# A cross-attention and mixture-of-experts block: inputs laid out turned, LayerNorms and routing placed inside the attention, expert chunks unrolled

## The chip, the cores and the metric

One core of one Trainium2 chip. A kernel is a fixed program of five engines: PE (TensorE, matmuls), DVE (VectorE), ACT (ScalarE), POOL (GpSimd) and SP (SyncE, which here issues the DMAs). The metric is the device time of one execution in microseconds (us), smaller is better.

## The reference, cut to what matters

```
x: (16, 256, 128)   ctx: (16, 1601, 96)   16 heads of 64, E = 32 experts, top 4
n   = layernorm(x)
q,k,v = n @ Wq, ctx @ Wk, ctx @ Wv                  # per head
x   = x + softmax(q k^T / 8) v @ Wo + bo
t   = layernorm(x)                                  # 4096 tokens
s   = sigmoid(t @ router_weight.T)
c   = s + router_bias; the best 2 of 4 groups (sum of their two largest), then the best 4 experts
w   = s[chosen] / sum(s[chosen]) * 2.5
x   = x + sum_e w[e] * down_e(silu(gate_e t) * up_e t) + shared expert
```

## The kernel before, in words

All of it is fp32; products that need precision are made of three fp32r matmuls, each operand being split into a high part (`hi`, a copy rounded to fp32r) and the rest (`lo`, full minus high). Wq and Wk are multiplied into one matrix A (128 x 96) per head, Wv and Wo into one matrix B, so that scores are n A ctx^T.

*Head.* x and the first two batches' keys are loaded; PE turns (transposes) the keys and the weights, makes A and B, DVE takes the LayerNorm of all 32 token tiles (lines 979 to 1003), and the 32 maxima tiles of the first group are made (L577) and reduced (L1038).

*Attention.* 64 groups (16 batches x 4 groups of 4 heads, 1024 queries). A group has 13 key tiles ("steps"). At step t PE makes the scores of tile t (6 matmuls of 512 columns, L608 to L614), then side jobs, then the weighted values of tile t-2 (6 matmuls, L623 to L629), then side jobs. ACT takes two exponentials of each score tile (L875, L878), and the rest `p_lo` (L282, two inputs in SBUF) is taken by DVE, at steps 3, 5, 7 and 9 by POOL. A side job fills one of only two PSUM banks (`side`) and DVE (or ACT and DVE) empties it: PE may fill a bank for job j only when job j-2 has been drained (`s_drain`). The table `SLOTS` sets the order: M, 32 maxima tiles of the group to come (L577, 402 columns; DVE reduces each, L1038); C, a quarter of the next batch's keys turned (L526, split by ACT L813 and DVE L1013); Y, a head's output projected (L637) and added to x1 (L1053, L1058); T, the maxima turned; Q, queries of a later group. Each engine's stream is in order. POOL also copies and splits A and x for a coming group (L421 to L430) and the values (L438, L440).

*Transition.* After the attention the expert weights are loaded, DVE and ACT take the second LayerNorm, PE turns the tokens (L520) and makes the router logits (L716), then 51 weight matrices are turned (L734) and split (L925, L1228), with the routing of chunk 0 (L1157 to L1218) in between.

*Expert chunks.* 8 chunks of 512 tokens, a loop over 17 pairs of experts q (the first is the shared expert). For each, PE makes gate and up (3 matmuls each, L745 to L747), spreads the routing weights (L790) and makes `down(q-2)` (3 matmuls, each of these 512 columns); ACT takes silu (L949), DVE two products (L1260, L1263), ACT `h_hi` (L932), POOL `h_lo` (L503), which `down` waits for. `hid`, `h_hi` and `h_lo` have three slots. DVE also routes the next chunk between the products at q = 5, 7, 9, 11, 13 and 15; PE turns these weights at the start of the next chunk (L768).

Of the kernel before, what the change touches and what calls it, by code (L numbers as in the profile page):

```python
# [10 lines left out]
I32 = mybir.dt.int32  # L29
# [8 lines left out]
def xattn_moe(nc, x, ctx, Wq, Wk, Wv, Wo, bo, router_w, router_b, gate_w, up_w, down_w,  # L38
              sh_gate_w, sh_up_w, sh_down_w, out):
    B, NQ, D = x.shape  # L40
    _, NC, DC = ctx.shape
    INNER = Wq.shape[1]
    DH = 64
    H = INNER // DH
    E, EI, _ = gate_w.shape
    SCALE = float(DH) ** -0.5
    assert D == P and NQ == 2 * P and H == 16 and EI * 2 == P and sh_gate_w.shape[0] == P
# [8 lines left out]
    QT = 4  # L56
    SPAD = NGB * QT
    MAXW = 402
    DOUBLES = 4 * MAXW - NC
    NM = 4 * (GQ // P)  # L60
    T = B * NQ // P
    NCH = T // 4
    NP = E // 2 + 1
    YW = D + 1
    OW = DC + 1

    stack = ExitStack()
    with stack:
# [6 lines left out]

        x1 = sb(stack, "x1", [P, T + 2, D])
        ident = sb(stack, "ident", [P, P])
        bo_rows = sb(stack, "bo_rows", [P, D])
        stats = sb(stack, "stats", [P, T, 6])
        mean = sb(stack, "mean", [P, T])  # L80
        dif = sb(stack, "dif", [P, T])
        var = sb(stack, "var", [P, T])
        std = sb(stack, "std", [P, T])
        rstd = sb(stack, "rstd", [P, T])
        xn = sb(stack, "xn", [P, 2, 4, D])
        recip = sb(stack, "recip", [P, 2])


        att = ExitStack()
        xnT = sb(att, "xnT", [P, (B + 1) * NQ])  # L90
        A_all = sb(att, "A_all", [P, H, DC])
        B_all = sb(att, "B_all", [OW, H, YW])
        A_hi = sb(att, "A_hi", [P, GH, DC], F32R)
        A_lo = sb(att, "A_lo", [P, GH, DC], F32R)
        x_hi = sb(att, "x_hi", [P, NQ], F32R)
        x_lo = sb(att, "x_lo", [P, NQ], F32R)
        pool_spare = sb(att, "pool_spare", [P, 1])
        nat = sb(att, "nat", [P, 2, SPAD, DC])
        c_stage = sb(att, "c_stage", [P, QT, DC])
        cT_hi = sb(att, "cT_hi", [OW, 2, SPAD * P], F32R)  # L100
        cT_lo = sb(att, "cT_lo", [DC, 2, SPAD * P], F32R)
        v_hi = sb(att, "v_hi", [P, 2, SPAD, OW], F32R)
        v_lo = sb(att, "v_lo", [P, 2, SPAD, OW], F32R)
        qT_hi = sb(att, "qT_hi", [OW, 2, GQ], F32R)
        qT_lo = sb(att, "qT_lo", [DC, 2, GQ], F32R)
        qT_max = sb(att, "qT_max", [DC, GQ], F32R)
# [3 lines left out]
        oT = sb(att, "oT", [OW, GQ])  # L110
        with ExitStack() as early:
            Wq_sb = sb(early, "Wq_sb", [P, INNER])
            Wk_sb = sb(early, "Wk_sb", [DC, INNER])
            Wv_sb = sb(early, "Wv_sb", [DC, INNER])
            Wo_sb = sb(early, "Wo_sb", [P, INNER // P, D])
            WT = sb(early, "WT", [P, 2, 3, P])
# [5 lines left out]

        moe = stack.enter_context(ExitStack())
        x2T_hi = sb(moe, "x2T_hi", [P, T * P], F32R)
        x2T_lo = sb(moe, "x2T_lo", [P, T * P], F32R)
        x2T_f = sb(moe, "x2T_f", [P, 2, BANK])
        w_nat = sb(moe, "w_nat", [P, 3, NP, P])
        gu_hi = sb(moe, "gu_hi", [P, 2, NP, P], F32R)
        gu_lo = sb(moe, "gu_lo", [P, 2, NP, P], F32R)
        d_hi = sb(moe, "d_hi", [P, NP, P], F32R)  # L130
        d_lo = sb(moe, "d_lo", [P, NP, P], F32R)
        rw_nat = sb(moe, "rw_nat", [E, D])
        rwT = sb(moe, "rwT", [P, E])
        rb_rows = sb(moe, "rb_rows", [P, E])
        before = sb(moe, "before", [P, N_EGROUP, N_EGROUP])
        sel_plain = sb(moe, "sel_plain", [P, E // 2, P])
        sel = sb(moe, "sel", [P, E // 2, P], F32R)
        score = sb(moe, "score", [P, T + 4, E])
        choice = sb(moe, "choice", [P, 4, E + TOP_K])
        struck = sb(moe, "struck", [P, 4, E + TOP_K])  # L140
        top8 = sb(moe, "top8", [P, 4 * N_EGROUP, 8])
        best8 = sb(moe, "best8", [P, 4, 8])
        g_sum = sb(moe, "g_sum", [P, 4, N_EGROUP])
        g_more = sb(moe, "g_more", [P, 4, N_EGROUP, N_EGROUP])
        g_same = sb(moe, "g_same", [P, 4, N_EGROUP, N_EGROUP])
        g_keep = sb(moe, "g_keep", [P, 4, N_EGROUP])
        ra = sb(moe, "ra", [P, 4, E])
        sigmoid = sb(moe, "sigmoid", [P, 4, E])
        spare = sb(moe, "spare", [P, 1])
        r1 = sb(moe, "r1", [P, 4])  # L150
        w_cat = sb(moe, "w_cat", [P, 4, P])
        w_r = sb(moe, "w_r", [P, 4, E], F32R)
        wT = sb(moe, "wT", [P, T * P], F32R)
        act_g = sb(moe, "act_g", [P, 2, BANK])
        gu_mul = sb(moe, "gu_mul", [P, 2, BANK])
        hid = sb(moe, "hid", [P, 3, BANK])
        h_hi = sb(moe, "h_hi", [P, 3, BANK], F32R)
        h_lo = sb(moe, "h_lo", [P, 3, BANK], F32R)
        yT = sb(moe, "yT", [P, BANK])

# [5 lines left out]
        s_x = sem("x_landed")  # L166
        s_w = sem("attn_weights_landed")
        s_nat = [sem("context_landed_even"), sem("context_landed_odd")]
        s_id = sem("identity_ready")
        s_set = sem("padding_preset")  # L170
        s_pset = sem("constants_preset")
# [47 lines left out]
        s_si = sem("gate_activated")  # L219
        s_hd = sem("hidden_made")  # L220
# [1088 lines left out]
```

## Time and profile before

| | us |
|---|---|
| median of 3 runs | 3518.87 (3518.13 to 3519.88) |
| the profiled execution | 3519.92 |
| its span, first to last instruction | 3518.1 |
| PE busy | 3410.5 |
| DVE busy | 2505.3 |
| ACT busy | 2027.8 |
| POOL busy | 1163.7 |

The program runs on one core, so the profile shows the whole time but 1.8 us. Busy shares are averages over stages that have different limits; the stages are read one by one from windows of the trace. "PEclk" is the clock granted to TensorE as a share of the full one.

### The profile page before, as it was taken

What the parts mean: (1) busy time and instruction counts of PE and PEld (TensorE: products, weight loads), DVE (VectorE), ACT (ScalarE), POOL (GpSimd) and SP (SyncE); (2) the same over time, 40 slices, a digit from 0 to 9 for tenths busy, and PEclk for the clock granted to TensorE, in tenths of its full rate; (3) what the DMA queues carried; (4) which work ended last, traced back from release to release, by engine and by line L of the source; (5) the groups of instructions that cost most, each with busy time, mean ns of one, the idle gap of its engine ahead of it and who ended that gap; (6) DMA issues with size and microseconds to landing.
All of it is one profiled execution on the core that took longest, in us unless ns stands there. A gap on an engine that the chain in (4) does not pass through costs nothing.

```text
span 3518.1 us, 54934 instructions
## 1 busy us (share of the span) xinstructions
PE 3410.5 (97%) x15929; PEld 2660.0 (76%) x15929; DVE 2505.3 (71%) x4705; ACT 2027.8 (58%) x2452; POOL 1163.7 (33%) x953
## 2 busy tenths in 40 slices
PE   6999999999999999999999999999999999979888
PEld 4777777777777777777777777777777777766665
DVE  5777776776776777677777767777767767778887
ACT  3566666566556666665666665665666665544443
POOL 3333332333333332323333332333333323324444
PEclk9999999999999999999999999999999999979999
DMA  2000000000000000000000000000000000020000
GB/s 67 0 0 8 0 8 0 8 0 8 0 8 0 8 0 8 0 8 0 3 5 0 8 0 8 0 8 0 8 0 8 0 8 0 3 37 6 6 6 6
DMA packets 18022, 22.31 MB, mean 6 GB/s; under 512 B 2976, under 2 KB 14280, under 8 KB 17928
## 3 DMA queue, kind: packets, MB, share of 16 engines
q1 hardware_dynamic: 17928, 20.86, 2.2%
q8 instruction: 83, 1.36, 0.2%
q14 instruction: 11, 0.09, 0.0%
HBM read 18.49 MB, written 2.10 MB: 6 GB/s over the span
## 4 chain that ended last, share of the span: by engine, by line
PE 83%; issue 8%; POOL 5%; DVE 2%; ACT 1%; DVEq 0%; POOLq 0%; DMA 0%; SPq 0%; ACTq 0%
PE side L577 12%; PE op L623 11%; PE op L629 11%; PE op L626 11%; PE st L608 10%; PE st L611 10%; PE st L614 10%; POOL h_lo L503 5%; PE side L637 3%; DVE cT_lo L1013 1%; PE side L569 1%; PE side L526 1%; PE side L571 1%; PE side L570 1%; ACT cT_hi L813 1%
## 5 line engine op out<-in xcount | busy, mean ns | idle before, releaser
L1038 DVE TENSOR_REDUCE m_part<-side 128x1 f32<-128x402 f32 x2064 | 1105.0, 571 | 513.1 <-PE side L577 503.0
L875 ACT ACTIVATE p_full<-st 128x1024 f32<-128x1024 f32 (+1 forms) x832 | 855.7, 1028 | 911.8 <-PE st L614 911.8
L282 POOL TENSOR_TENSOR p_lo<-p_full,p_hi 128x1024 fp32r<-128x1024 f32 x256 | 657.6, 2569 | 1060.6 <-ACT p_hi L878 1060.6
L282 DVE TENSOR_TENSOR p_lo<-p_full,p_hi 128x1024 fp32r<-128x1024 f32 (+1 forms) x576 | 717.9, 1246 | 220.3 <-ACT p_hi L878 220.3
L878 ACT ACTIVATE p_hi<-st 128x1024 fp32r<-128x1024 f32 (+1 forms) x832 | 853.7, 1026 | 0.0
L577 PE MATMUL side<-cT_hi,qT_max 96*128 96x402 f32 x2064 | 619.5, 358 | 7.4 <-DVE qT_lo L1032 2.0
L608 PE MATMUL st<-qT_hi,cT_hi 97*128 (+3 forms) x1668 | 540.6, 405 | 1.9 <-ACT p_hi L878 1.0
L623 PE MATMUL op<-p_hi,v_hi 128*97 128x512 f32 (+1 forms) x1664 | 526.4, 397 | 0.0
L611 PE MATMUL st<-qT_lo,cT_hi 96*128 (+3 forms) x1668 | 524.9, 396 | 0.0
L629 PE MATMUL op<-p_hi,v_lo 128*97 128x512 f32 (+1 forms) x1664 | 520.6, 394 | 0.0
L626 PE MATMUL op<-p_lo,v_hi 128*97 128x512 f32 (+1 forms) x1664 | 520.6, 394 | 0.0
L577 PEld LDWEIGHTS side<-cT_hi,qT_max 96*128 96x128 f32 x2064 | 389.4, 189 | 173.3 <-DVE cT_lo L1013 28.3
L614 PE MATMUL st<-qT_hi,cT_lo 96*128 (+3 forms) x1668 | 518.4, 392 | 0.0
L611 PEld LDWEIGHTS st<-qT_lo,cT_hi 96*128 96x128 f32 (+1 forms) x1668 | 308.9, 185 | 79.5
L614 PEld LDWEIGHTS st<-qT_hi,cT_lo 96*128 96x128 f32 (+1 forms) x1668 | 306.6, 184 | 80.7
L629 PEld LDWEIGHTS op<-p_hi,v_lo 128*97 128x97 f32 (+1 forms) x1664 | 269.8, 162 | 116.3 <-issue 0.2
L626 PEld LDWEIGHTS op<-p_lo,v_hi 128*97 128x97 f32 (+1 forms) x1664 | 269.7, 162 | 114.9
L608 PEld LDWEIGHTS st<-qT_hi,cT_hi 97*128 97x128 f32 (+1 forms) x1668 | 295.9, 186 | 31.3 <-issue 4.5
L623 PEld LDWEIGHTS op<-p_hi,v_hi 128*97 128x97 f32 (+1 forms) x1664 | 266.1, 164 | 29.5
L503 POOL TENSOR_TENSOR h_lo<-hid,h_hi 128x512 fp32r<-128x512 f32 x136 | 175.0, 1287 | 251.7 <-ACT h_hi L932 250.3
L434 POOL COPY c_stage<-nat 128x384 f32 (+1 forms) x68 | 34.8, 512 | 650.7 <-PE side L571 642.4
L813 ACT ACTIVATE cT_hi<-side 96x512 f32 (+1 forms) x68 | 40.3, 594 | 257.0 <-PE side L526 257.0
(182 smaller groups left out, 3242.2 us busy)
## 6 DMA issues: line engine op xcount, KB each, us to landing
nat<-in_ctx SPq DMA_DIRECT2D x18, 576.0 KB
out_x<-x SPq DMA_DIRECT2D x8, 256.0 KB, 2.3
qT_hi<-m_row SPq DMA_DIRECT2D x65, 4.0 KB
w_nat<-in_L_ffn_gate_w SPq DMA_DIRECT2D x2, 512.0 KB, 7.2
w_nat<-in_L_ffn_up_w SPq DMA_DIRECT2D x2, 512.0 KB, 9.4
Wq_sb<-in_L_xattn_Wq SPq DMA_DIRECT2D x1, 512.0 KB, 6.2
Wo_sb<-in_L_xattn_Wo SPq DMA_DIRECT2D x1, 512.0 KB, 9.4
nat<-in_ctx SPq DMA_DIRECT2D x18, 24.4 KB
```

Of the source, the lines that this page charges most:

```text
L282: eng.tensor_tensor(p_lo[0:m, slot(s), :], p_full[0:m, s % 2, :], p_hi[0:m, slot(s), :].bitcast(F32), ALU.subtract).then_inc(s_lo_pool if ...
L503: pool.tensor_tensor(h_lo[:, q % 3, :], hid[:, q % 3, :], h_hi[:, q % 3, :].bitcast(F32), ALU.subtract).then_inc(s_hl, 1)
L577: pe.matmul(where[:, 0:MAXW], qT_max[:, tile * P:(tile + 1) * P], cT_hi[0:DC, par, part * MAXW:(part + 1) * MAXW], start=True, stop=True). ...
L608: pe.matmul(st[0:m, s % 2, j, :], cT_hi[:, par, keys], qT_hi[:, i % 2, halves[j]], start=True, stop=False)
L611: pe.matmul(st[0:m, s % 2, j, :], cT_hi[0:DC, par, keys], qT_lo[:, i % 2, halves[j]], start=False, stop=False)
L614: mm = pe.matmul(st[0:m, s % 2, j, :], cT_lo[:, par, keys], qT_hi[0:DC, i % 2, halves[j]], start=False, stop=True)
L623: pe.matmul(op[0:OW, j, :], v_hi[0:m, par, s, :], p_hi[0:m, slot(s), halves[j]], start=(s == 0), stop=False)
L626: pe.matmul(op[0:OW, j, :], v_hi[0:m, par, s, :], p_lo[0:m, slot(s), halves[j]], start=False, stop=False)
L629: mm = pe.matmul(op[0:OW, j, :], v_lo[0:m, par, s, :], p_hi[0:m, slot(s), halves[j]], start=False, stop=(s == S - 1))
L875: act.activation(p_full[0:m, s % 2, :], both(st[0:m, s % 2]), ACT.Exp, scale=SCALE)
L878: act.activation(p_hi[0:m, slot(s), :], both(st[0:m, s % 2]), ACT.Exp, scale=SCALE).then_inc(s_ex, 1)
L1038: dve.tensor_reduce(m_part[:, k:k + 1], where[:, 0:MAXW], AX.X, ALU.max).then_inc(s_drain, 1)
```

## The change

The function is rewritten in many places. What is computed stays the same.

- *Layout.* The host passes x as 128 x 32 x 128, the keys twice (plain, and turned with seven keys repeated so that four pieces of 402 columns hold them), the attention weights and the expert weights already turned and side by side, and takes the output in the layout of x1.
- *Head.* Only the first two token tiles are normalised there. A is made for all heads and split once (`A_hi`, `A_lo` for 16 heads), so POOL stages no A later. The first maxima are made in pairs of banks and reduced two at a time, with the products of later heads in between. No keys and no weights are turned on PE.
- *Attention.* `qT_max` is gone: maxima use `qT_hi`. Keys of the next batch come turned; POOL copies and splits them with the values (`split_piece`, four instructions a group). The C job is replaced by `EXTRA`: nothing in group 0, L (turn the next batch's two token tiles) in group 1, N (turn two token tiles for the second LayerNorm, those of the batch before) in group 2, R (router logits) in group 3. DVE gets `between(t)`: statistics in groups 0 and 1 at t = 7, normalising in groups 1 and 2 at t = 3, the routing of 256 tokens in group 3 at t = 6, 7, 8 and 10. The root of the variance is taken by POOL (`pow`). ACT's part of the extra job stands behind exp(5) rather than ahead of it. All engines' loops hold 8 groups unrolled.
- *Transition.* Only the last batch's second LayerNorm and its logits are left; the first five experts' weights were loaded before the attention loop.
- *Expert chunks.* Fully unrolled, `down` is made three experts late (`down(g - 3)`), four slots (`hslot`), no routing on DVE but that of the last 256 tokens in chunk 1. In chunk 0, ACT and DVE split one expert's three matrices (128 x 384) at each q, two ahead. The routing weights of the next chunk are turned at q = 10.

```diff
-        SLOTS = {2: ("MM", "M"), 3: ("MM", "M"), 4: ("MM", "MM"), 5: ("MM", "MC"), 6: ("MM", "MM"),
+        PLACES = {2: ("MM", "M"), 3: ("MM", "M"), 4: ("MM", "MM"), 5: ("MM", "MX"), 6: ("MM", "MM"),
...
+        EXTRA = ("", "L", "N", "R")
...
+            def split_piece(bb, par, i):
...
+                pool.tensor_copy(cT_hi[0:DC, other, cols], keys_tur[:, cols])
+                pool.tensor_copy(v_hi[:, other, tiles, 0:DC], keys_nat[:, tiles, :]).then_inc(s_sh, 1)
...
+                pool.tensor_tensor(cT_lo[:, other, cols], keys_tur[:, cols],
+                                   cT_hi[0:DC, other, cols].bitcast(F32), ALU.subtract)
+                pool.tensor_tensor(v_lo[:, other, tiles, 0:DC], keys_nat[:, tiles, :],
+                                   v_hi[:, other, tiles, 0:DC].bitcast(F32), ALU.subtract).then_inc(s_v, 1)
...
+            def token_stats(tiles, base=0):
+                for q in range(2):
+                    ins = dve.bn_stats(stats[:, q, :], x1[:, tiles[q], :])
+                link(ins, base)
+                carry()
+                for q in range(2):
+                    ins = dve.bn_aggr(moments[:, q, :], stats[:, q, :])
+                link(ins, base)
+                dve.tensor_scalar(var_eps[:, :], moments[:, :, 1], EPS, None, ALU.add).then_inc(s_var, 1)
+
+            def normalise(tiles, count):
+                dve.wait_ge(s_rstd, count)
+                for q in range(2):
+                    ins = dve.tensor_scalar(xn[:, q, :], x1[:, tiles[q], :], moments[:, q, 0:1], rstd[:, q:q + 1],
+                                            ALU.subtract, ALU.mult)
...
+            def add_one(count):
+                dve.wait_ge(s_ls, count)
+                dve.tensor_scalar(ra[:, :, :], ex[:, :, :], 1.0, None, ALU.add).then_inc(s_drain, 1)
...
+            def route_groups(base=0):
+                flat = g_sum[:, :, :].rearrange("p t g -> p (t g)")
+                link(dve.tensor_tensor(flat, top8[:, :, 0], top8[:, :, 1], ALU.add), base)
...
+                def between(t):
+
+                    if i == 0 and t == 7:
+                        token_stats([dve.snap(bb * 4 + (2 * par + 4 + q)) for q in range(2)], links)
+                    elif i == 1 and t == 3:
+                        normalise([dve.snap(bb * 4 + (2 * par + 4 + q)) for q in range(2)], bb * 4 + (2 * par + 2))
+                    elif i == 1 and t == 7:
+                        token_stats([dve.snap(bb * 4 + (2 * par + q)) for q in range(2)], links)
+                    elif i == 2 and t == 3:
+                        normalise([dve.snap(bb * 4 + (2 * par + q)) for q in range(2)], bb * 4 + (2 * par + 3))
+                    elif i == 3 and t == 6:
+                        route_scores(jobs + (job_at[i]["R"][0] + 1), links)
+                    elif i == 3 and t == 7:
+                        route_groups(links)
+                    elif i == 3 and t == 8:
+                        route_experts(links)
+                    elif i == 3 and t == 10:
+                        route_weights(bass.ds(bb * 4 + 2 * par, 2), links)
+
+                at = places(i)
                 lo(0)
                 for t in range(2, S):
-                    side_jobs(SLOTS[t][0])
+                    side_jobs(at[t][0])
                     lo(t - 1)
                     if t == S - 1:
                         lo(t)
-                    side_jobs(SLOTS[t][1])
+                    between(t)
+                    side_jobs(at[t][1])
...
+            for c in range(NCH):
                 for q in range(NP):
-                    w = (q - 1) % NP
...
+                    if g >= 3:
+                        down(g - 3)
```

## Rows read from the trace of the kernel before

**Rows 1.** The page, first part: busy time of each engine.

```profile
PE 3410.5 (97%) x15929; PEld 2660.0 (76%) x15929; DVE 2505.3 (71%) x4705; ACT 2027.8 (58%) x2452; POOL 1163.7 (33%) x953
```

**Rows 2.** Windows by stage: us, busy of PE, PEld, DVE, ACT, POOL, clock.

```profile
0.00:79.10 79.10, 48.55 (x194) 33.45 (x194) 41.92 (x115) 22.89 (x70) 28.87 (x37) 1.00 0.23 67
79.10:3070.60 2991.50, 2984.35 (x14157) 2340.36 (x14158) 2110.02 (x3746) 1816.24 (x2052) 951.01 (x768) 1.00 0.01 4
3070.60:3129.50 58.90, 35.16 (x169) 30.94 (x169) 41.41 (x133) 22.50 (x43) 8.80 (x12) 0.61 0.34 57
3129.50:3518.10 388.60, 342.41 (x1414) 255.25 (x1412) 311.99 (x712) 166.16 (x288) 174.98 (x136) 0.98 0.02 6
```

**Rows 3.** Waits of the whole span: total us, times, longest.

```profile
PEld side L577 <- DVE cT_lo L1013: 28.3, 64, 0.5
PEld side L577 <- DVE m_part L1038: 27.4, 111, 0.3
```

**Rows 4.** Chain of waits in one attention group: start, us, what.

```profile
1544.02 0.44 PE side L526 x4
...
1545.86 0.18 PE side L577
...
1546.08 0.45 PE side L577
```

**Rows 5.** Timeline of DVE in two attention groups.

```profile
1503.21 1.06 DVE L1038 TENSOR_REDUCE m_part<-side 128x1 f32<-128x402 f32 x2 [0.70 <-PE side L577]
1504.19 1.50 DVE L282 TENSOR_TENSOR p_lo<-p_full,p_hi 128x1024 fp32r<-128x1024 f32 x1
...
1536.40 1.21 DVE L282 TENSOR_TENSOR p_lo<-p_full,p_hi 128x1024 fp32r<-128x1024 f32 x1
```

**Rows 6.** Timeline of POOL, attention and transition.

```profile
1503.86 0.74 POOL L430 TENSOR_TENSOR x_lo<-xnT,x_hi 128x256 fp32r<-128x256 f32 x1
1505.12 2.81 POOL L282 TENSOR_TENSOR p_lo<-p_full,p_hi 128x1024 fp32r<-128x1024 f32 x1 [0.53 <-ACT p_hi L878]
...
1537.34 2.53 POOL L282 TENSOR_TENSOR p_lo<-p_full,p_hi 128x1024 fp32r<-128x1024 f32 x1 [4.87 <-ACT p_hi L878]
...
3077.39 4.47 POOL L493 TENSOR_SCALAR_AFFINE_SELECT sel_plain<-sel_plain 128x2048 f32<-128x2048 f32 x2
```

**Rows 7.** Single lines: instructions, ns min/median/max, first and last start, forms.

```profile
L1170 DVE TENSOR_TENSOR g_sum<-top x9: 186/944/944, 3118.0 to 3482.4; 128x16 f32<-128x16 f32 x9
...
L1003 DVE TENSOR_SCALAR xn<-x,mean,rstd x64: 335/341/348, 39.1 to 3103.8; 128x128 f32 x64
...
L1214 DVE CAST w_r<-ra x9: 217/862/867, 3128.0 to 3505.0; 128x128 fp32r<-128x128 f32 x9
...
L768 PE MATMUL op<-ident,w_cat x32: 272/273/447, 3128.8 to 3460.4; 128*128 128x128 f32 x32
```

**Rows 8.** Timeline of DVE between attention and expert chunks.

```profile
3074.71 0.87 DVE L979 BATCH_NORM_STATS2 stats<-x 128x6 f32<-128x128 f32 x4
...
3079.87 2.03 DVE L990 TENSOR_SCALAR var<-var 128x32 f32<-128x32 f32 x1
...
3120.03 0.23 DVE L1180 TENSOR_TENSOR g_more<-g_more,g_same 128x64 f32<-128x64 f32 x1
3120.29 0.22 DVE L1181 TENSOR_REDUCE g_keep<-g_more 128x16 f32<-128x64 f32 x1
```

**Rows 9.** Chain of waits in the head: start, us, what.

```profile
54.96 0.21 PE side L570
...
60.00 15.57 DVE m_part L1038 x32
```

**Rows 10.** Timeline of PE in the expert chunks and at the end.

```profile
3137.30 0.39 PE L745 MATMUL st<-x2T_hi,gu_hi 128*128 128x512 f32 x1
...
3139.59 0.39 PE L745 MATMUL st<-x2T_hi,gu_hi 128*128 128x512 f32 x1
...
3510.72 0.79 PE L745 MATMUL op<-h_hi,d_hi 128*128 128x512 f32 x1 [2.65 <-POOL h_lo L503]
```

More of the change, by code:

```diff
@@ L28 @@
 F32R = mybir.dt.float32r
-I32 = mybir.dt.int32
 P = 128
@@ new lines, in project_queries @@
+            def project_queries(where, g, half, k):
+                for h in range(2):
+                    head = g * GH + 2 * k + h
+                    o = where[0:DC, h * NQ:(h + 1) * NQ]
+                    pe.matmul(o, A_hi[:, head, :], x_hi[:, half, :], start=True, stop=False)
+                    pe.matmul(o, A_hi[:, head, :], x_lo[:, half, :], start=False, stop=False)
+                    mm = pe.matmul(o, A_lo[:, head, :], x_hi[:, half, :], start=False, stop=True)
+                mm.then_inc(s_fill, 1)
@@ L604, in scores @@
+            pe.wait_ge(s_mc, 1)
+            pe.wait_ge(s_drain, J0_T - 1)
+            turn_maxima(bank(J0_T))
+            def scores(s, slot, par):
                 m = rows(s)
@@ L664, in side_jobs @@
                         k = made[kind]
-                        j = job_at[kind][k]
+                        j = job_at[i][kind][k]
                         made[kind] += 1
+                        where = bank(jobs0 + j)
                         pe.wait_ge(s_drain, jobs + (j - 1))
@@ new lines, in _ @@
+            for k in range(2):
+                queries_lo(bank(J0_Q + k), k + 1, k, 0)
+            for u in range(NM // 2):
+                where = (st[:, 0], st[:, 1], op)[u % 3]
+                tile, part = u % (NM // 4), u // (NM // 4) * 2
+                if u == NM // 2 - 2:
+                    for k in range(2):
+                        queries_lo(bank(J0_Q1 + k), k + 3, k, 1)
+                dve.wait_ge(s_mx, u + 1)
+                dve.tensor_reduce(m_part[:, tile * 4 + part:tile * 4 + part + 2], where[:, :, 0:MAXW], AX.X,
+                                  ALU.max).then_inc(s_mxd, 1)
@@ L1239, in _ @@
-            keep_weights(None)
+                    between(t)
+                    side_jobs(at[t][1])
+            links_per_turn = 48
+            with dve.Fori(0, B // 2) as bb:
+                for par in range(2):
+                    for i in range(NGB):
+                        body(bb, par, i)
+            assert steps[0] - head_steps == links_per_turn, steps[0] - head_steps
+            steps[0] = head_steps + B // 2 * links_per_turn
+            for h in range(GH):
+                dve.wait_ge(s_drain, JOBS_END + h)
+                add_head(bank(JOBS_END + h), JOBS_END + h + 1, NG * GH + h + 1, (T, T + 1))
@@ L1282, in body @@
-                per_chunk[0] = steps[0] - start
-            per_chunk = [0]
-            chunks(dve, body)
+                    if c == 1:
+                        if q == 8:
+                            route_scores(JOBS_END + GH + 2)
+                        elif q == 10:
+                            route_groups()
+                        elif q == 12:
+                            route_experts()
+                        elif q == 14:
+                            route_weights(slice(T, T + 2))
@@ L1297 @@
     from concourse.bass_utils import run_bass_kernel_spmd
[L1299 to L1305 removed]
+    take = lambda name: np.asarray(inputs[name])
@@ new lines @@
+    flat = lambda a: np.ascontiguousarray(a, dtype=np.float32)
+    x, ctx = take("x"), take("ctx_768")
+    Wq, Wk, Wv, Wo = (take("L0_xattn_" + n) for n in ("Wq", "Wk", "Wv", "Wo"))
+    gate, up, down = (take("L0_ffn_" + n) for n in ("gate_w", "up_w", "down_w"))
+    shared = [take("L0_ffn_shared_" + n) for n in ("gate_w", "up_w", "down_w")]
+    keys = np.zeros((16, 13 * P, 96), np.float32)
+    keys[:, 0:1601] = ctx
+    attn_w = np.concatenate([Wq.T.reshape(8, P, P), Wk.T.reshape(8, P, 96), Wv.T.reshape(8, P, 96),
+                             Wo.reshape(8, P, P)], axis=2)
```

1407 lines of the change are left out of this document (641 added, 766 removed).

## The prediction

> **What bounds the kernel now.** I read the page's busy times first: PE is busy 97% of the span [rows 1]. The windows by stage say where it isn't: the head takes 79.1 us, the attention 2991.5, the transition 58.9 and the expert chunks 388.6 [rows 2]. In the attention PE is busy 2984 of 2991 us, one group of the 64 taking 2991.5/64 = 46.74. There every stall of PE is lost time and every matmul saved is won. The waits and the chain show three small stalls per group: the C job (28.3/64 = 0.44, behind DVE's cT_lo) and a late DVE reduction (27.4/64 = 0.43 [rows 3]), besides one for the heads that stays. So DVE, at 2110 us busy, is nearly in the way at some steps though its share is only 71%.
>
> **Head.** Before, DVE's 32 reductions take 15.6 us and end at 75.6; scores start at 79.1 [rows 2, 9]. After, only two tiles are normalised, the keys and weights come turned. I walk it: data at about 4, statistics and root to 5.7; normalising, turning and splitting to 10 (2.8 later if POOL's long memset of a constant row blocks DVE, which I take at half); A and the first queries to 16; then PE, not DVE, bounds the maxima: 32 tiles of 402 columns at 0.21 us per 256 [rows 9] are 10.7, three rounds of weight products 6.3, the second queries 2.6; then 3.5 to 4.5 for the maxima's row, as now (79.1 - 75.6). Together 41.0 (37 to 46): **38.1 saved**. The products' 2.1 a round is an estimate from the same rate.
>
> **Attention, work of PE.** C costs 0.44 of PE [rows 4] and its stall 0.44 (the pair behind it takes 0.45 where two singles of 0.18 would do, and waits once more [rows 4]). The stall by the late reduction has a cause: DVE's p_lo of step 6 takes 1.50 instead of 1.21 because POOL's x_lo runs until 1504.6 [rows 5, 6]; POOL no longer stages x, so 0.30 goes. A bare group is 46.74 - 0.45 - 0.44 - 0.30 = 45.55. L and N add 0.23 each (two turns of 128 columns), R about 0.45: a batch is 4 x 45.55 + 0.91 = 183.1, before 187.0. POOL's four key copies lie beside PE, and their neighbours on DVE read PSUM.
>
> **Attention, DVE's new work.** This is where it is decided. With two banks, PE's second M of a pair waits until DVE has drained the pair's forerunner. Between two pairs PE has 6 x 0.23 = 1.39 of other matmuls, a pair lasts 0.37: half a step is 1.76. DVE needs 1.06 for a pair [rows 5] and 1.21 for a p_lo, which on even t stands with POOL or nowhere and on odd t makes 2.27 in one half and 1.06 in the other. On odd t the slack behind p_lo is about 0.2; on even t it is 1.1. What `between` adds beyond that stalls PE one for one.
>
> What its pieces cost: small operations with a wait start 0.26 apart [rows 8], 0.24 at half size. Statistics: two at 0.24 (0.87 for four [rows 8]), a memset, two aggregations at about 0.15 (no row; 0.1 to 0.3), one tensor_scalar: 1.2. Groups of the routing: 7 operations, 1.7. Scores of the routing 1.6, experts 1.15, weights 1.9 (their forms for four tiles, each reduced to two). Normalising: 0.55.
>
> On top comes a lock. g_sum takes 0.19 alone and 0.94 in the median case, when POOL is in its h_lo [rows 7]; a tensor_scalar that takes 0.18 alone took 2.03, until POOL's select had ended (3077.39 + 4.47 = 3081.86 [rows 6, 8]). So such operations wait for the end of POOL's instruction. In the attention POOL's p_lo lasts 2.4 to 2.8. At t = 3 and 7 it becomes ready while DVE is in its own p_lo: 1537.34 against an end at 1537.5, 1505.12 against 1505.6 [rows 5, 6]. POOL thus goes first, and what DVE has next waits 2.4.
>
> - Group 3, t = 7, route_groups: g_sum waits to 10.2 after scores(6) began, the last of seven ends at 11.9, the reduction at 12.45, while PE wants its bank at 8.9: 3.6, and 0.3 for the second, **3.9**. Certain kind of wait: the very operation is in the rows.
> - Group 3, t = 6, 8 and 10: 0.45 + 0 + 0.5; and add_one, a tensor_scalar, behind p_lo(5): 0.7 more. With t = 7: **5.5** (4.8 without the lock on add_one).
> - Groups 0 and 1, t = 7, statistics: the last tensor_scalar waits for p_lo(7): 2.35 each (1.0 without): **4.7**.
> - Groups 1 and 2, t = 3, normalising: 2.3 each (0 without): **4.6**. Is it an operation that waits? It takes 0.335 [rows 7]. A copy of as many elements takes 0.217, which waits (0.86 [rows 7]); two scalars from memory at about 0.06 each (an estimate) bring 0.217 to 0.335. A pass at one element a cycle would give 0.40. I take it as one that waits.
>
> Sum 14.8 a batch (4.3 if nothing waited). After: 16 x (183.1 + 14.8) = 3166.4, **174.9 more** than 2991.5.
>
> What the rows show is that DVE waits for POOL's instruction to end. The Trainium skill, SBUF — State Buffer, section Who interferes with whom, speaks against this change: VectorE and GpSimd share a port pair under an exclusive lock, taken by copy, cast and tensor_scalar in their two-port mode and by operations with two SBUF inputs against a GpSimd instruction that reads SBUF. The trace agrees (2.03 and 0.94 above). By this rule both the statistics' last operation and normalising would wait, which is the sum here; had the rule only held for two tensor inputs, the sum would be that of the second rival.
>
> **Transition.** Of 58.9 [rows 2] only the last batch is left: heads added 4.1, statistics and root 1.5, normalising between POOL's memset and x2_lo 2.7, turns, logits and routing turn 3.2 at the slow clock: 11.5 (9 to 14). **47.4 saved.** The first weights are there; the rest has 6 us before its first use.
>
> **Expert chunks.** Chunks start (3460.4 - 3128.8)/7 = 47.4 apart [rows 7], but an undisturbed step takes 3139.59 - 3137.30 = 2.29 [rows 10]: 17 steps and two turns of 0.45 are 39.7. The rest is DVE's routing, late products, and `down` waiting for h_lo. The routing goes and `down` is a step later, so PE bounds: from the gate of a step to h_lo takes 5.3, `down` now comes at 8.5. In chunk 0 ACT has 1.7 and DVE 1.9 per step against 2.29: covered, if DVE's splitting fits ahead of POOL's h_lo (0 to 10 if not). 136 steps 309, turns 6, slow clock at the start 2, less three late downs 2, end of the last step to the last byte 11, stalls in chunks 0 and 1 3: 329 (324 to 338). **59.6 saved.**
>
> **The sum.** 41.0 + 3166.4 + 11.5 + 329.0 = 3547.9 against a span of 3518.1: +29.8. The profiled execution is 3519.92, 1.8 above its span; the median 3518.87 is 1.05 lower. Forecast 3518.9 + 29.8 = 3548.7, own range 3520 to 3580.
>
> **Rivals.**
> 1. *Normalising does not wait* (one port, or DVE gets it first; the margin at t = 3 is 0.2 us [rows 5, 6]). 16 x 4.6 = 73.6 less: 3475, faster. It decides from half that gain on: with a stall under 0.4 per piece the kernel is no slower. Chance 0.20.
> 2. *No one-source operation waits*, or PE's slack is larger than I read: stalls 6.8 instead of 14.8, 128 less: 3421; with no lock at all, 3381. For it: only two such rows met POOL's select, none its p_lo. Chance 0.19.
> 3. *The long stalls bring TensorE's clock down.* After 2.65 idle a matmul of 512 columns takes 0.79 instead of 0.39 [rows 10]; the 3.9 of group 3 is longer, though ahead of it PE is dense. Eleven matmuls 0.2 later each are 2.3 a batch: 3586. Chance 0.13.
> 4. *The expert chunks don't get shorter*, DVE or ACT taking PE's place: 8 x 7.7 more, 3610. Against it: DVE's 1.4 and ACT's 1.2 a step. Chance 0.04.
>
> **Numbers.** The forecast's case has 0.44. Range 3435 to 3600: it leaves out most of rival 2 and rival 4. A measurement can tell about 0.2%, 7 us. Slower by more: most of 0.44 (0.36), 0.13, 0.04: 0.53. Same: 0.05. Faster: 0.19, 0.20 and 0.03 of the forecast's own case: 0.42.
>
> **What would show it.** Right: groups 0 to 3 of a batch of about 47.9, 50.4, 48.1 and 51.5 us; DVE's xn at t = 3 and var_eps near 2.4 us long, g_sum up to 2.4; PE's waits for m_part some 230 us in all; chunks 39.7 apart; scores at 41. Wrong: xn at 0.34 throughout, or waits for m_part under 100 us; a head over 46.

## The result, and the profile after

The changed kernel takes 3603.57 us (median of 4 runs, 3602.96 to 3609.24), the kernel before 3518.5 beside it: a ratio of 1.0245 (95% interval 1.0228 to 1.0263), so 2.3 to 2.6% slower. The forecast was 3548.7, its range 3435 to 3600. The profiled execution has a span of 3600.8 us and takes 3602.96. Its page, first the busy line, then the chain that ended last:

```profile
span 3600.8 us, 50491 instructions
...
PE 3386.3 (94%) x15589; PEld 2655.2 (74%) x15589; DVE 2578.8 (72%) x4960; ACT 1935.5 (54%) x2239; POOL 1076.8 (30%) x737
...
PE 77%; DVE 11%; issue 9%; POOL 1%; DVEq 0%; ACT 0%; POOLq 0%; DMA 0%; ACTq 0%
```

PE's share fell from 97% [rows 1] to 94%, and it is busy 24 us less: the change did take work off PE, and gave more idle time back. The windows by stage say where (head, attention, transition, chunks; columns as in [rows 2]):

```profile
0.00:38.30 38.30, 20.47 (x124) 16.34 (x124) 23.48 (x34) 10.51 (x18) 25.60 (x31) 0.96 0.51 171
38.30:3265.00 3226.70, 3042.74 (x14029) 2375.06 (x14030) 2343.36 (x4576) 1750.46 (x1905) 863.06 (x560) 0.97 0.03 8
3265.00:3275.80 10.80, 4.66 (x27) 3.60 (x27) 8.85 (x27) 3.50 (x9) 2.85 (x3) 0.79 0.56 218
3275.80:3600.80 325.00, 318.42 (x1414) 260.21 (x1412) 203.16 (x324) 171.06 (x308) 185.24 (x143) 0.99 0.02 7
```

| us | before | forecast | after | after minus forecast |
|---|---|---|---|---|
| head | 79.1 | 41.0 | 38.3 | -2.7 |
| attention | 2991.5 | 3166.4 | 3226.7 | +60.3 |
| transition | 58.9 | 11.5 | 10.8 | -0.7 |
| expert chunks | 388.6 | 329.0 | 325.0 | -4.0 |
| span | 3518.1 | 3547.9 | 3600.8 | +52.9 |

Three stages gained 152.5 us and the attention lost 235.2. All that the forecast missed lies in the attention. There a batch of four groups looks like this (windows from one group's first scores to the next one's; columns: length, PE busy, PEclk, DMA share and GB/s):

```profile
240.00:288.30 48.30, 46.39 (x219) 1.00 0.00 1
288.30:339.70 51.40, 47.75 (x220) 0.97 0.00 1
339.70:387.70 48.00, 46.00 (x220) 1.00 0.04 13
387.70:441.40 53.70, 49.68 (x222) 0.94 0.05 14
```

Over all 16 batches the four groups take 48.1, 51.6, 48.0 and 53.8 in the mean, where the forecast had 47.9, 50.4, 48.1 and 51.5. Groups 0 and 2 are right to 0.2. Groups 1 and 3 are 1.2 and 2.3 longer, and they are the two in which the granted clock is below 1.

**The lock is there as forecast.** DVE in group 1 at t = 7, with POOL beside it:

```profile
314.84 1.21 DVE L1004 TENSOR_TENSOR p_lo<-p_full,p_hi 128x1024 fp32r<-128x1024 f32 x1
315.97 0.48 DVE L848 BATCH_NORM_STATS2 stats<-x 128x6 f32 x2
316.49 0.18 DVE L852 BATCH_NORM_AGGREGATE moments<-stats 128x2 f32<-128x6 f32 x1
...
316.77 1.54 DVE L854 TENSOR_SCALAR var_eps<-moments 128x2 f32<-128x2 f32 x1
...
315.77 2.51 POOL L383 TENSOR_TENSOR p_lo<-p_full,p_hi 128x1024 fp32r<-128x1024 f32 x1 [4.56 <-ACT p_hi L745]
```

POOL's p_lo ends at 315.77 + 2.51 = 318.28, var_eps at 316.77 + 1.54 = 318.31. The statistics run beside POOL at their usual pace; the tensor_scalar on two elements per partition doesn't. The same holds for the other pieces (a line's durations in ns, least/median/most):

```profile
L859 DVE TENSOR_SCALAR xn<-x,moments,rstd x68: 334/1616/2880, 5.3 to 3271.2; 128x128 f32 x64, 128x128 f32<-128x128 f32 x4
L854 DVE TENSOR_SCALAR var_eps<-moments x34: 169/1537/1544, 3.8 to 3269.9; 128x2 f32<-128x2 f32 x34
L917 DVE TENSOR_TENSOR g_sum<-top x17: 433/2349/2354, 213.1 to 3340.2; 128x8 f32<-128x8 f32 x17
L901 DVE TENSOR_SCALAR ra<-ex x17: 195/1881/1890, 205.1 to 3275.6; 128x64 f32<-128x64 f32 x17
```

**The low clock is what the forecast had left to a rival.** The same stretch of PE's stream, first in group 0 (the stall before it as long), then in group 1:

```profile
268.57 0.94 PE L449 MATMUL side<-cT_hi,qT_hi 96*128 96x402 f32 x2 [1.67 <-DVE m_part L1016]
269.35 0.63 PE L513 MATMUL op<-p_hi,v_hi 128*97 128x512 f32 x2
269.82 0.63 PE L516 MATMUL op<-p_lo,v_hi 128*97 128x512 f32 x2
270.29 0.63 PE L519 MATMUL op<-p_hi,v_lo 128*97 128x512 f32 x2
```

```profile
318.84 1.19 PE L449 MATMUL side<-cT_hi,qT_hi 96*128 96x402 f32 x2 [1.66 <-DVE m_part L1016]
319.82 1.05 PE L513 MATMUL op<-p_hi,v_hi 128*97 128x512 f32 x2
320.67 1.05 PE L516 MATMUL op<-p_lo,v_hi 128*97 128x512 f32 x2
321.53 0.88 PE L519 MATMUL op<-p_hi,v_lo 128*97 128x512 f32 x2
```

Pairs that start 0.47 apart in group 0 start 0.85 apart in group 1: about half speed, 1.2 instead of 2.4 GHz by the granted clock of 0.51 below. The windows of the two places in groups 1 and 3, and one right behind the first (PEclk is the figure after the count):

```profile
318.60:322.00 3.40, 3.16 (x8) 0.51 0.00 0
322.00:325.40 3.40, 3.40 (x19) 0.99 0.00 0
...
417.60:424.40 6.80, 5.68 (x16) 0.50 0.00 0
```

So a low stretch of 3.4 us in group 1 and one of 6.8 us in group 3, in each of the 16 batches. The first begins where a stall ends (318.6, the next matmul at 318.8), the second 1.1 us before its stall of 2.9 is over (417.6 against 418.7).

### The profile page after: what moved, and what is told of

It reads as the page before. It is cut to its first block, busy times and chain, and to the rows that moved or that the text cites. A ratio compares the mean times of both kernels' runs of the same rounds, so it can differ in the third digit from the quotient of the medians.

```text
span 3600.8 us, 50491 instructions
## 1 busy us (share of the span) xinstructions
PE 3386.3 (94%) x15589; PEld 2655.2 (74%) x15589; DVE 2578.8 (72%) x4960; ACT 1935.5 (54%) x2239; POOL 1076.8 (30%) x737
## 4 chain that ended last, share of the span: by engine, by line
PE 77%; DVE 11%; issue 9%; POOL 1%; DVEq 0%; ACT 0%; POOLq 0%; DMA 0%; ACTq 0%
PE side L449 10%; PE op L513 9%; PE op L516 9%; PE st L499 9%; PE op L519 9%; PE st L502 9%; PE st L505 9%; PE side L525 3%; DVE m_part L1016 3%; DVE p_lo L1004 3%; PE st L614 2%; PE st L612 2%; PE st L613 2%; DVE xn L859 1%; DVE g_sum L917 1%
## 5 line engine op out<-in xcount | busy, mean ns | idle before, releaser
L449 PE MATMUL side<-cT_hi,qT_hi 96*128 96x402 f32 x2048 | 613.1, 364 | 178.5 <-DVE m_part L1016 165.0
L449 PEld LDWEIGHTS side<-cT_hi,qT_hi 96*128 96x128 f32 x2048 | 395.0, 193 | 344.6 <-DVE m_part L1016 220.2
L499 PE MATMUL st<-qT_hi,cT_hi 97*128 97x512 f32 (+1 forms) x1668 | 548.3, 410 | 3.2 <-DMA qT_hi<-m_row 3.0
L513 PE MATMUL op<-p_hi,v_hi 128*97 128x512 f32 (+1 forms) x1664 | 540.4, 407 | 0.0
L516 PE MATMUL op<-p_lo,v_hi 128*97 128x512 f32 (+1 forms) x1664 | 533.0, 402 | 0.0
L519 PE MATMUL op<-p_hi,v_lo 128*97 128x512 f32 (+1 forms) x1664 | 532.3, 402 | 0.0
L502 PE MATMUL st<-qT_lo,cT_hi 96*128 96x512 f32 (+1 forms) x1668 | 529.5, 398 | 0.0
L505 PE MATMUL st<-qT_hi,cT_lo 96*128 96x512 f32 (+1 forms) x1668 | 523.4, 395 | 0.0
L525 PEld LDWEIGHTS side<-B_all,oT 97*128 97x128 f32 x1040 | 153.7, 200 | 28.8 <-DVE m_part L1016 12.2
L892 DVE SCALAR_TENSOR_TENSOR x<-side,recip,x 128x128 f32 (+1 forms) x520 | 158.5, 347 | 11.1 <-DVE recip L889 2.5
```

What stands on the lines that cost most here:

```text
L449: return pe.matmul(where[:, 0:MAXW], qT_hi[0:DC, slot, tile * P:(tile + 1) * P], cT_hi[0:DC, par, part * MAXW:(part + 1) * MAXW], start=Tr ...
L499: pe.matmul(st[0:m, s % 2, j, :], cT_hi[:, par, keys], qT_hi[:, slot, halves[j]], start=True, stop=False)
L502: pe.matmul(st[0:m, s % 2, j, :], cT_hi[0:DC, par, keys], qT_lo[:, slot, halves[j]], start=False, stop=False)
L505: mm = pe.matmul(st[0:m, s % 2, j, :], cT_lo[:, par, keys], qT_hi[0:DC, slot, halves[j]], start=False, stop=True)
L513: pe.matmul(op[0:OW, j, :], v_hi[0:m, par, s, :], p_hi[0:m, slot(s), halves[j]], start=(s == 0), stop=False)
L516: pe.matmul(op[0:OW, j, :], v_hi[0:m, par, s, :], p_lo[0:m, slot(s), halves[j]], start=False, stop=False)
```

## The experiments

Two theories stood after this. *Lock and clock:* the stalls come of DVE's operations that wait for POOL's p_lo, their size is as forecast, and each long one brings PE's clock down, which costs the missing 3.8 a batch. The rival: *load*, DVE simply has too much to do at those steps, or the surplus lies in the bare batch. All group times below are means over the 16 batches of the profiled execution. Executions of one kernel with such stalls differ (norm_at_4: 3497.8 to 3512.9 us with mean granted clocks of 0.985 to 0.989; the profiled one took longest, at 0.985), so a count "of 16" is that of one execution.

### no_pieces: the bare batch

```diff
                 def between(t):
+                    if (i, t) in ((0, 7), (1, 7)):
+                        dve.memset(spare[:, :], 0.0).then_inc(s_var, 1)
+                    elif (i, t) in ((1, 3), (2, 3)):
+                        dve.wait_ge(s_rstd, bb * 4 + (2 * par + (i + 1)))
+                        dve.memset(spare[:, :], 0.0).then_inc(s_xn, 1)
+                    elif (i, t) == (3, 10):
+                        dve.memset(spare[:, :], 0.0).then_inc(s_rw, 1)
+                    return
```

> Work left out: statistics, normalising and routing of all batches but the first and the last inside the attention (the operations between the steps), with constant routing weights in their place; PE's and ACT's jobs for them stay. This measures the bare batch. Theory (bare batch 183.1, 0.7 for the add_one that still waits): attention 16 x 183.8 = 2941, whole 3603.6 - 3226.7 + 2941 = 3318, and no stretch of low clock after the head. Rival (PE's slack was misread, a part of the surplus is in the bare batch): a batch of 185 to 187, 3337 to 3370.

Measured: 3331.66 us. One batch, its four groups:

```profile
406.40:452.40 46.00, 45.77 (x219) 1.00 0.01 2
452.40:498.10 45.70, 45.70 (x220) 1.00 0.00 1
498.10:543.80 45.70, 45.70 (x220) 1.00 0.05 12
543.80:590.80 47.00, 46.19 (x223) 1.00 0.06 18
```

In the mean 45.9 + 45.7 + 45.7 + 47.0 = 184.3, where the theory had 183.8, and no low clock. The attention takes 16 x 184.3 and 4.2 at its end, 2954 instead of 2941, so the forecast's removals from PE (C, its stall, the late p_lo) are right within 0.5 a batch, and 17.1 of the 201.4 of a batch of the changed kernel are the pieces' doing (their stalls and the low clock behind them). Group 3's 47.0 is R (0.45 forecast) and the add_one that waits (0.7): together 1.3 over the others.

### var_by_sum: one operation in another form

```diff
-                dve.tensor_scalar(var_eps[:, :], moments[:, :, 1], EPS, None, ALU.add).then_inc(s_var, 1)
+                dve.tensor_reduce(var_eps[:, :], moments[:, :, 1:3], AX.X, ALU.add).then_inc(s_var, 1)
```

with EPS in a third column of `moments`.

> One operation in its old place, in another form: the variance plus epsilon by a tensor_reduce over the pair (variance, epsilon) instead of a tensor_scalar. Theory 1 (a tensor_scalar waits for the end of POOL's p_lo, a reduction doesn't): var_eps takes about 0.2 instead of 1.54, the long step of groups 0 and 1 falls from 5.97 and 7.3 to about 4.6, and group 1's stretch of low clock, if it hangs on the length of that stall, goes too: 16 x (1.4 + 1.4) = 45 less, 3559, or 3538 without the low clock. Rival A (DVE has too much to do behind its p_lo, whatever the form): no change, 3603. Rival B (any operation of DVE on SBUF waits for POOL): no change, and the reduction itself is about 1.5 long.

Measured: 3563.39 us, ratio to before 1.0124 (1.0102 to 1.0146).

```profile
L854 DVE TENSOR_REDUCE var_eps<-moments x34: 156/157/158, 3.8 to 3224.3; 128x2 f32<-128x4 f32 x34
```

From 1.54 to 0.16 in the same place, beside the same POOL instruction: it is the form of the operation, not DVE's load and not the mere company of POOL. Group 0 went from 48.1 to 46.8; its long step from 5.95 to 4.61, as expected. The stall left at t = 7 is 0.9 and brings no low clock in any of the 32 groups 0 and 1. But the stall at t = 3, unchanged at 2.3, which had brought none, now does so in 4 of 16 groups 1 and in 13 of 16 groups 2, which take 49.2 instead of 48.0. That wasn't expected, and is why 3538 wasn't reached.

### norm_at_4 and stats_at_8: each half alone

```diff
-                    elif i == 1 and t == 3:
+                    elif i == 1 and t == 4:
...
-                    elif i == 2 and t == 3:
+                    elif i == 2 and t == 4:
```

> Normalising goes from t = 3 to t = 4, where DVE has no p_lo and POOL's has ended; nothing else. Theory 1 (lock): xn is 0.34 long throughout, the long step of groups 1 and 2 falls from 5.8 to 3.6 at most, 16 x 2 x 2.2 = 70 less: 3533. Rival A (DVE's own load): the stall shrinks only by p_lo's share, 0.67 - 0.2 each: 16 x 2 x 0.5 = 15 less, 3588. On the clock: if the low stretch in group 1 at t = 7 needs the stall at t = 3 before it, it goes and another 16 x 1.3 = 21 go with it (3512); if the stall at t = 7 is enough, it stays (3533).

Measured: 3503.02 us, 0.9948 of before (0.9931 to 0.9964). Two of the eight pieces that `between` places in a batch, 0.67 us each, were moved by one step: that alone turns a loss of 2.4% into a gain of 0.5%. xn's median is 0.34:

```profile
L859 DVE TENSOR_SCALAR xn<-x,moments,rstd x68: 335/341/2880, 5.4 to 3181.0; 128x128 f32 x64, 128x128 f32<-128x128 f32 x4
```

Groups: 48.5, 48.3, 45.7 and 53.0; group 2 is a bare one again, group 1 has low clock in 4 batches instead of 16 (group 0 in 3 instead of none), and group 3's low stretch is 3.4 us in 14 batches (52.9) and 6.8 in two (54.0). Load alone would have given 3588. The time is 9 us under the lower of the theory's two figures, 3512, since it had no change in group 3; why that stretch got shorter is open.

```diff
-                    if i == 0 and t == 7:
+                    if i == 0 and t == 8:
...
-                    elif i == 1 and t == 7:
+                    elif i == 1 and t == 8:
```

> The mirror of norm_at_4: only the statistics of groups 0 and 1 go from t = 7 to t = 8, normalising stays at t = 3, group 3 as in the changed kernel. Theory (lock): var_eps takes 0.17, the long steps at t = 7 of groups 0 and 1 go, the ones at t = 3 of groups 1 and 2 stay at 5.8: groups of 45.9, 48.0, 48.0 and 53.8, 16 x (2.1 + 3.6) = 91 less than 3603.6: 3513. On the clock: group 1 has one stall of 2.3 then and group 2 one. If low clock in group 1 wants two stalls in one group, neither has it (3513); if a single stall of this length can bring it, as delay_only's did in 11 of 16 batches, up to 16 x 1.5 to 3.0 more (3537 to 3560).

Measured: 3536.39 us, at the lower end of the second alternative (3537). var_eps takes 0.17 and group 0 is at 45.9: the lock's part came as expected. On the clock, one stall of 2.3 in group 1 brings it down in 14 of 16 batches, one in group 2 in 6 of 16. "Two stalls in one group" is refuted as the condition. What it gives is a clean price, the same group with and without low clock (two batches of this run, group 1; then two of group 3, with a low stretch of 3.4 and of 6.8 us):

```profile
88.30:136.30 48.00, 46.02 (x220) 1.00 0.00 1
284.20:333.70 49.50, 47.50 (x220) 0.97 0.00 1
...
579.10:631.90 52.80, 48.80 (x222) 0.97 0.05 15
184.30:238.20 53.90, 49.92 (x222) 0.94 0.05 14
```

49.5 against 48.0: 1.5 us for a stretch of 3.4. The other runs give the same: 49.53 against 47.96 (var_by_sum, group 2), 49.43 against 47.86 (delay_only, group 1). In group 3 the 9 batches with a stretch of 3.4 take 52.8 and the 7 with one of 6.8 take 53.8: the longer one costs 1.0 more, so about 2.5 in all.

### delay_only: idle time without a lock

To no_pieces is added:

```diff
+                        if i == 1:
+                            for k in range(20, 31):
+                                dve.bn_stats(scratch[:, k, :], x1[:, 2, :])
...
+                    elif (i, t) == (3, 7):
+                        for k in range(20):
+                            dve.bn_stats(scratch[:, k, :], x1[:, 2, :])
```

> Work left out as in no_pieces (statistics, normalising and routing of the batches in the attention); in their place DVE does dummy bn_stats in a row at t = 7, which wait for nothing: 11 in group 1 (11 x 0.245 = 2.7) and 20 in group 3 (4.9). Does PE's idle time alone bring its clock down, without any lock? Theory (it does): PE stalls by 2.5 and 4.7, and behind that the low clock costs as in the changed kernel, 2.3 to 3.6 a batch: a batch of 184.3 + 7.2 + 2.3 to 3.6, group 3 at 53 to 54, whole 3331 + 16 x (9.5 to 10.8) = 3483 to 3504. Rival (the low clock belongs to the lock, to POOL or to code loading): no low stretch, 3331 + 16 x 7.2 = 3446.

Measured: 3474.31 us. Groups 45.9, 48.9, 45.7 and 53.0; low clock in 11 of 16 groups 1 and in all groups 3. Two groups 1 of this run:

```profile
85.20:133.00 47.80, 46.20 (x220) 1.00 0.00 1
277.10:326.50 49.40, 47.80 (x220) 0.97 0.00 1
```

In group 1 no operation of DVE waits for POOL and none of `between`'s pieces is left (in group 3 add_one still waits, as in no_pieces): PE idle for some 2 us inside dense work is enough to bring its clock down. The whole is 9 us under the expected range, since 11 bn_stats stalled PE by 2.1, not 2.5, and 20 by about 3.9, not 4.7 (52.4 with a low stretch of 3.4, less 1.5 and 47.0), and 5 groups kept their clock.

### group3_left and even_steps: towards a better kernel

group3_left has both moves above (t = 3 to 4, 7 to 8).

> Statistics at t = 8 and normalising at t = 4 as in even_steps; group 3 (scores at 6, groups at 7, experts at 8, weights at 10) as in the changed kernel. It separates the terms of group 3 from the others' and from their clock. Theory: groups 0 to 2 as in even_steps (45.9, 45.75, 45.7); group 3 has 47.0 + 4.4 for route_groups + 0.8 for the others = 52.2 without and about 53 to 53.7 with low clock; 3346 + 16 x 4.5 to 5.9 = 3418 to 3440. If the low clock in group 3 comes from the earlier stalls of groups 1 and 2, it goes (3418); if route_groups' own stall of over 3 us is enough, it stays (3430 to 3440).

Measured: 3441.47 us. Groups 45.9, 45.8, 45.7 and 53.8:

```profile
516.90:562.60 45.70, 45.70 (x220) 1.00 0.05 12
562.60:616.60 54.00, 50.02 (x223) 0.94 0.05 15
```

Group 3 keeps its full length and its 6.8 us of low clock with no stall ahead of it in groups 0 to 2: the stall of route_groups (up to 3.4 us of idle time on PE's weight loads) is enough by itself. The run without it is even_steps, where group 3 has no low stretch.

even_steps moves group 3's pieces too, and the router's turn with them:

```diff
-        PLACES = {2: ("MM", "M"),
+        PLACES = {2: ("MM", "MZ"),
...
-        EXTRA = ("", "L", "N", "R")
+        EXTRA = ("", "L", "N", "")
+        EARLY = ("", "", "", "R")
...
-                    elif i == 3 and t == 6:
+                    elif i == 3 and t == 4:
                         route_scores(jobs + (job_at[i]["R"][0] + 1), links)
-                    elif i == 3 and t == 7:
+                    elif i == 3 and t == 6:
                         route_groups(links)
```

> The whole work, with every piece at an even t, where POOL's p_lo is over and DVE has none of its own: statistics at t = 8, normalising at t = 4, the router's turn at t = 2, and scores, groups, experts, weights of the routing at t = 4, 6, 8, 10 of group 3. Theory (lock, slack of 1.1 at even t): stalls of 0.1 + 0.1 (statistics), 0.5 + 0.6 + 0.1 + 0.8 (routing) = 2.2 a batch instead of 14.8 and no low clock: a batch of 185.3, attention 2965, whole 3342 (3325 to 3370), faster than both kernels. Rival A (a piece costs its own length wherever it stands): 10.1 a batch, 3318 + 16 x 10.1 = 3480.

Measured: 3346.28 us, 0.9511 of before (0.9495 to 0.9527): 4.9% faster than the kernel before, 7.1% faster than the changed one (3346.28/3603.57). A batch takes 185.4 (46.0, 45.8, 45.7 and 47.9), where the slack that the forecast had read for even steps gave 185.3, and the clock stays full from 42.8 us, early in the first group, to the end of the attention. The operations that waited are short now:

```profile
L861 DVE TENSOR_SCALAR xn<-x,moments,rstd x68: 335/341/2881, 5.3 to 3012.5; 128x128 f32 x64, 128x128 f32<-128x128 f32 x4
L856 DVE TENSOR_SCALAR var_eps<-moments x34: 168/169/176, 3.7 to 3011.2; 128x2 f32<-128x2 f32 x34
L919 DVE TENSOR_TENSOR g_sum<-top x17: 160/165/436, 196.6 to 3081.5; 128x8 f32<-128x8 f32 x17
```

### spread: finer, and worse

The router's turn at t = 10 of group 2; in group 3 scores at 2, groups in two parts at 4 and 6, experts at 8, weights in two parts at 10 and 12.

> even_steps with the routing cut finer: the router's turn at t = 10 of group 2, then in group 3 scores at t = 2, the first three operations of the groups at 4, the other four at 6, experts at 8, the first five of the weights at 10, the last three at 12. Theory: what exceeds the slack of an even step in even_steps (a batch takes 1.0 to 1.1 more than the bare one there, 184.3 to 185.4) goes by half or more: 16 x 0.6 = 10 less, 3336 (3328 to 3344). Rival (those steps are late by DVE's whole load in group 3, or POOL and t = 12 are in the way): 3346 or more.

Measured: 3382.34 us, 0.9612 of before (0.9596 to 0.9628): 36 slower than even_steps, where 10 faster was expected. Group 2 takes 46.9 (step t = 10 got 1.1 longer by the router's turn), group 3 48.9 (in 2 of 16 batches a low stretch follows, 50.4 against 48.7). DVE in group 3, with POOL beside it:

```profile
558.21 1.21 DVE L1018 TENSOR_TENSOR p_lo<-p_full,p_hi 128x1024 fp32r<-128x1024 f32 x1
559.34 0.54 DVE L907 RECIPROCAL sigmoid<-ra 128x64 f32<-128x64 f32 x1
...
560.95 1.70 DVE L1030 TENSOR_REDUCE m_part<-side 128x1 f32<-128x402 f32 x3
562.56 3.38 DVE L1018 TENSOR_TENSOR p_lo<-p_full,p_hi 128x1024 fp32r<-128x1024 f32 x1
...
562.47 2.39 POOL L384 TENSOR_TENSOR p_lo<-p_full,p_hi 128x1024 fp32r<-128x1024 f32 x1 [20.16 <-ACT p_hi L746]
```

t = 2 is even but not empty: DVE takes p_lo of step 1 there and that of step 2 right after, at t = 3. The scores push the second behind POOL's p_lo of step 3, which begins 0.09 earlier, and DVE's own p_lo takes 3.38 instead of 1.21. A piece can lose the race for an operation that stands behind it.

### The expert chunks: before_no_routing and down_earlier

Routing left out of the kernel before (its calls at q = 5 to 13):

> The kernel before, with the routing of chunks 1 to 7 left out of the expert chunks (work left out: every chunk takes the weights of chunk 0); all else as before. It says how much of the 47.4 a chunk took before was DVE's routing. Theory (PE bounds a chunk once the routing is gone, and down a step earlier costs what it did in down_earlier): 40.7 to 41.2 a chunk, 7 x 6.5 = 46 less than 3518.9: 3473. Rival (routing costs what it costs in chunk 1 of the changed kernel, 2.2 for half the tiles, so 4.4, and the rest is the rolled loop and its waits): 43 a chunk, 3488.

Measured: 3457.27 us, 0.9821 of before (0.9792 to 0.9849), a larger gain than either expected. The product of the shared expert, once a chunk, in this kernel and in the changed one:

```profile
L1266 DVE TENSOR_TENSOR hid<-st,act_g x8: 691/692/692, 3133.3 to 3408.9; 128x512 f32<-128x512 f32 x8
```

```profile
L1117 DVE TENSOR_TENSOR hid<-st,act_g x8: 681/692/692, 3278.6 to 3554.9; 128x512 f32<-128x512 f32 x8
```

(3408.9 - 3133.3)/7 = 39.4 and (3554.9 - 3278.6)/7 = 39.5 a chunk. So leaving out DVE's routing gains all of the 7.9 a chunk, with `down` still two steps behind: the later `down` isn't needed for it on the kernel before.

```diff
-                    if g >= 3:
-                        down(g - 3)
+                    if g >= 2:
+                        down(g - 2)
```

> The expert chunks alone: down follows two steps behind its gate, as in the kernel before, instead of three. Theory of the prediction (from the gate to h_lo takes 5.3, an undisturbed down at two steps comes at about 6.2, so only disturbed steps are late): chunks without routing stay at 39.5, chunk 0 and chunk 1 (with the last batch's routing, 41.75) grow by 1 to 4: 3603 to 3610. Rival (the step more was what the change's chunks gained): 39.5 grows toward 45, 3603 + 6 x 5 = 3633 or more.

Measured: 3618.41 us, a ratio of 1.028 (1.026 to 1.0301), 15 above the changed kernel. Chunks 4 to 7 start 40.7 apart instead of 39.5: neither of the two expected figures. PE's own wait in one of them (PE waited for, us in total, times, longest):

```profile
PEld op L612 <- ACT yT L811: 1.2, 1, 1.2
```

It isn't h_lo: the next chunk's first `down` now comes before ACT has copied the last chunk's output out of its bank (1.2, the whole of 40.7 - 39.5). Of the 16.8 by which its span is the longer one, 11.0 lie behind the attention; 3.0 lie in the head and 2.8 in the attention, whose code is the same (the last section says more of the head).

## Why the prediction was right and wrong

**Right, step by step.** The head's walk (41.0 against 38.3; xn takes 2.95 there behind POOL's memset, the 2.8 that was taken at half), the transition (11.5 against 10.8), and the chunks (329 against 325), with 39.7 forecast for a chunk and 39.5 measured, PE busy through all of it:

```profile
3396.40:3435.80 39.40, 39.40 (x179) 32.40 (x177) 23.52 (x35) 20.47 (x38) 23.29 (x18) 1.00 0.02 7
```

The bare batch: 183.1 + 0.7 forecast, 184.3 measured. The lock, which made the sign: normalising waits every time (rival 1 had 0.20 on the contrary), one-source operations wait down to two elements per partition (rival 2, 0.19). The stalls: 2.35 a piece for the statistics, 5.95 - 3.71 = 2.24 measured; 2.3 for normalising, 5.79 - 3.53 = 2.26 measured (the step's length in the changed kernel less that in no_pieces). var_eps is 1.54 long and not 2.4; the stall was right because it runs to the end of POOL's instruction and the reduction comes behind it. PE's waits for m_part:

```profile
PEld side L449 <- DVE m_part L1016: 220.2, 162, 3.4
```

against "some 230".

**Wrong: the clock.** The step that failed is that the sum had no term for TensorE's clock: it put it at nothing and left it to rival 3. This went wrong in two ways. First, rival 3 had a chance of 0.13 and no share in the forecast, though [rows 10] showed half speed after an idle time of 2.65 and the forecast itself had a stall of 3.9 in each batch. Its price for group 3, 2.3, was nearly right. Group 3 takes 53.8 in the changed kernel, with 6.8 us of low clock; with 3.4 us of it the group takes 52.8 to 52.9 (stats_at_8, norm_at_4), and 1.5 off gives 51.3. That last figure is worked out, since no run shows this group without low clock; it is near the forecast's 51.5, and the difference to 53.8 is 2.5. Second, the stalls of 2.3 were taken as too short to count. In group 1 one such stall brought the clock down in every batch of the changed kernel, 1.5 each. That is 4.0 a batch, 16 x 4.0 = 64 us, against the 60.3 by which the attention missed. The rest of the sum nearly cancels: the stalls came out 1.0 a batch lower than forecast (201.4 - 184.3 - 4.0 = 13.1 against 14.1 without add_one), the bare batch 0.5 higher, and the attention has 4.2 us at its end that the sum left out (64 - 16 + 8 + 4 = 60). Without low clock the four groups would stand at 48.1, 50.1, 48.0 and 51.3, the forecast's being 47.9, 50.4, 48.1 and 51.5.

**The chunks were right for half a reason.** Three causes were named for what a chunk of 47.4 takes over 39.7. before_no_routing shows that the first, DVE's routing, is enough to remove: what there was of the other two goes with it.

**The range.** Its lower part stood for rivals 1 and 2, both of which the durations of xn and var_eps rule out. Rival 1's threshold was also wrong: to bring the kernel back to the time before, normalising would have had to stall 29.8/16 = 1.9 a batch less, so 1.4 a piece instead of 2.3, not "under 0.4". The range's upper end was 3.6 short: it was the forecast's case with rival 3's one low stretch and some more, and there were two.

**What stays open:** which stalls of 2.1 to 2.3 bring the clock down, and when a longer one brings 3.4 and when 6.8 us of it. The same stall in the same place did so in 0 of 16 batches (the changed kernel's group 2), 6 (stats_at_8) and 13 (var_by_sum). Two in one group aren't needed (stats_at_8, 14 of 16 with one), and the lock isn't (delay_only, 11 of 16). The long stall of group 3 (3.2 to 3.7 us of idle time on PE's weight loads) did it in every batch of all seven kernels that had it, and the one of 0.9 at t = 7 (var_by_sum) in none.

## What to carry to other kernels

A piece of work moved to an engine with time to spare is priced by what its neighbour engine does at that very step: a 0.17 us tensor_scalar behind POOL's 2.5 us instruction stalled PE by 2.3, and by nothing one step later. So list, per step, who holds what, and place each piece where the long instruction of the other engine is over and the step has no work of its own kind behind it; here that, with the router's turn moved ahead of the pieces that need it, made 3604 into 3346. And where the sum has idle stretches of 2 us and more inside dense matmuls, add the clock as a term: up to 1.5 us for each of about 2 us, up to 2.5 for one of over 3.

## What the runs showed of the hardware

- Beside POOL's p_lo (two inputs in SBUF, 2.4 to 2.5 us), a tensor_scalar from SBUF of 2, 64 or 128 elements per partition waits to its end, and so do a tensor_tensor of 8 and DVE's own p_lo; bn_stats and bn_aggr in the same stretch, and a tensor_reduce in the tensor_scalar's place, don't. The Trainium skill, SBUF — State Buffer, section Who interferes with whom, names the shared port pair and its exclusive lock, and tensor_scalar among the operations that take it in their two-port mode; the trace agrees, by var_by_sum's 0.16 against 1.54.
- In the attention TensorE's low stretches are 3.4 or 6.8 us long, at half speed; one of 3.4 costs 1.5 us, one of 6.8 about 1.0 more (stats_at_8, group 3). Idle times of 1.6 to 2.0 us between matmuls, inside otherwise dense work, were followed by one in 0 to 16 of 16 batches, depending on the kernel around them; one of 1.3 still was in 2 of 16 (spread, group 3).
- The head's length differs between kernels whose head has the same code: scores start at 36.3 (even_steps, no_pieces, spread), 38.3 (the changed kernel), 41.1 (norm_at_4) and 42.6 (var_by_sum, with one memset more), with DVE at nearly the same times up to 16. From there PE sets the pace: four maxima tiles take 1.01 at 26.2 in the changed kernel, but 1.71 at 28.5 in var_by_sum, about half speed (here the changed kernel's row, then var_by_sum's):

```profile
26.23 1.01 PE L473 MATMUL st<-cT_hi,qT_hi 96*128 96x402 f32 x4
```

```profile
28.48 1.71 PE L473 MATMUL st<-cT_hi,qT_hi 96*128 96x402 f32 x4
```

So when PE comes to its full clock in a head full of small gaps differs from kernel to kernel by several us; that is why differences of up to 6 us between the whole times above are not explained one by one.
